# Three score banks and a fourth projection bank, with a new written order, in a cross-attention kernel

## What is computed

```python
q = x @ Wq + bq;  k = ctx @ Wk + bk;  v = ctx @ Wv + bv
scores = einsum('bkgld,bksd->bkgls', q, k) * HD ** -0.5 + mask
attn = softmax(scores, axis=-1)
out = einsum('bkgls,bksd->bkgld', attn, v)      # 8 key heads, 4 query heads each
x = out.reshape(b, l, 1024) @ Wo + bo + x
return (x - mu) * rsqrt(var + 1e-6) * gamma + beta
```

## Time and profile before

| | before |
|---|---|
| median of three executions | 1751.57 us |
| the profiled execution's own time | 1751.32 us |
| its span, first to last instruction | 1749.3 us |
| PE busy | 1602.6 us (92%) |
| DVE, ACT, POOL busy | 83%, 79%, 53% |
| mean granted clock of PE | 0.974 |
| batch 5, from PV 7 of batch 4 to its own PV 7 | 207.67 us |

### The profile page before, as it was taken

One profiled execution on the slowest core, in us unless ns is written; L12 is line 12 of the kernel. 1 busy time (PEld: TensorE's weight loads), 2 busy tenths in 40 slices (PEclk: granted clock), 3 DMA queues, 4 the chain that ended last, 5 costly groups with the idle time before them and its releaser, 6 DMA issues. The chain is left out here.

```text
span 1749.3 us, 38438 instructions
## 1 busy us (share of the span) xinstructions
PE 1602.6 (92%) x14048; PEld 1110.0 (63%) x14048; DVE 1448.7 (83%) x2773; ACT 1385.7 (79%) x3186; POOL 935.7 (53%) x731
## 2 busy tenths in 40 slices
PE   3898879999899989999899998999989999999986
PEld 2665556576566765676576775667666676667654
DVE  4489878789788996889888898789988899788886
ACT  3578868769888787978889789787888878887794
POOL 5426433526754458534675448662585545856382
PEclk8999999999999999999999999999999999999998
DMA  9669987646885578664796567965678646875331
GB/s 178 186 148 227 241 232 199 182 135 168 250 257 144 138 187 286 188 154 122 209 288 185 130 175 192 287 178 127 174 238 252 158 133 170 292 208 150 84 114 67
DMA packets 357292, 325.02 MB, mean 186 GB/s; under 512 B 145776, under 2 KB 248176, under 8 KB 357104
## 3 DMA queue, kind: packets, MB, share of 16 engines
q1 hardware_dynamic: 357104, 322.56, 67.5%
HBM read 244.85 MB, written 83.89 MB: 188 GB/s over the span
## 5 line engine op out<-in xcount | busy, mean ns | idle before, releaser
L1941 PE MATMUL bank<-ring_hi,w_sb 128*128 128x512 f32 x2368 | 785.5, 399 | 32.1 <-issue 19.2
L1725 ACT ACTIVATE probs<-probs,shift 128x512 f32<-128x512 f32 x1024 | 726.9, 713 | 92.1 <-DVE shift L1826 91.0
L1839 DVE STREAM_TRANSPOSE turned_p<-probs 128x2048 f32<-128x2048 f32 x256 | 585.7, 2297 | 154.3 <-PE bank L2021 149.3
L1826 DVE CUSTOM_DVE_ANT_0 probs<-bank,mask_l 128x512 f32<-128x512 f32 x1024 | 643.1, 680 | 56.3 <-PE bank L2001 37.2
L1626 POOL TENSOR_TENSOR w_sb<-w_raw,w_sb 128x512 fp32r<-128x512 f32 x320 | 412.1, 1297 | 413.8 <-ACT w_sb L1682 413.7
L1941 PEld LDWEIGHTS bank<-ring_hi,w_sb 128*128 128x128 f32 x2368 | 444.4, 189 | 149.9 <-issue 42.6
L1941 PE MATMUL bank<-ring_lo,w_sb 128*128 128x512 f32 x1184 | 467.9, 395 | 0.0
L2001 PE MATMUL bank<-k_stack,q_stack 96*128 96x512 f32 x1024 | 358.9, 414 | 12.7 <-DVE shift L1826 10.0
L2021 PE MATMUL bank<-turned_p,v_all 32*32 32x512 f32 x8192 | 307.9, 642 | 65.8 <-DVE turned_p L1839 48.6
L1638 POOL TENSOR_TENSOR ring_lo<-x_t,ring_hi 128x512 fp32r<-128x512 f32 x168 | 214.7, 1291 | 144.9 <-ACT ring_hi L1694 144.4
L2001 PEld LDWEIGHTS bank<-k_stack,q_stack 96*128 96x128 f32 x1024 | 186.1, 189 | 143.3 <-issue 62.9
(11 more groups left out here) (75 smaller groups left out, 933.2 us busy)
## 6 DMA issues: line engine op xcount, KB each, us to landing
w_raw<-w_d SPq DMA_DIRECT2D x144, 256.0 KB, 3.7
q_stack<-q_hi_d SPq DMA_DIRECT2D x128, 256.0 KB, 4.3
w_raw<-in_L_xattn_Wo_dram SPq DMA_DIRECT2D x128, 256.0 KB, 3.0
q_hi_d<-part_hi SPq DMA_DIRECT2D x64, 256.0 KB, 3.9
q_lo_d<-part SPq DMA_DIRECT2D x64, 256.0 KB, 5.0
...
v_all<-v_d SPq DMA_DIRECT2D x256, 64.0 KB, 2.2
...
```

The costliest lines, as they stand in the source:

```text
L1725: nc.scalar.activation(probs[:, st % 2, h, :], probs[:, st % 2, h, :], ACT.Exp, scale=-1.0, bias=shift[:, g % 2, i:i + 1], accum_out=sums[ ...
L1826: nc.vector.tensor_tensor_reduce(out=probs[:, st % 2, h, :], in0=S_ps[h][:, :], in1=mask_l[:, st, :], scale=-1.0, scalar=HIGHEST, op0=ALU. ...
L1839: nc.vector.transpose(turned_p[:, :, :, st, :].rearrange("p j h c -> p h j c"), probs[:, st % 2, :, :].rearrange("p h (j c) -> p h j c", c ...
L1941: mm = nc.tensor.matmul(C[c][:, :], w_sb[:, n_w, (1, 0, 0)[third], d % 4, :], (hi, lo, hi)[third], start=(n == 0), stop=(n == 23))
```

## The change

The PSUM banks are dealt out anew. Scores have three banks (0, 1, 2), used in turn by the running number, and score n waits for the DVE read of score n-3. Bank 3 becomes the projections' own. Projection tiles use bank 3 ("2" in `BANKS`) and, where a window has three or four tiles, bank 4 (and 5) for those in the middle. A window with two tiles has both in bank 3, one behind the other. A PV waits only for the `keep`s of tiles in banks 4 and 5. In the last batch the row products `e` use banks 1, 2, 0 in place of 0, 1, 2, and the last `rbc` uses bank 0 in place of bank 3. `WINDOWS` is unchanged, and each step's work is the same. Nearly every number in `BASE` and `PLACES` differs (about 1,770 lines of the diff), so that all engines have a new order.

```diff
-BASE = {1: 256.32, 2: 463.56, 3: 671.62, 4: 879.00, 5: 1086.39, 6: 1293.78, 7: 1501.17}
+BASE = {1: 252.03, 2: 464.77, 3: 672.77, 4: 880.77, 5: 1088.76, 6: 1296.76, 7: 1504.76}
...
+BANKS = {1: (2,), 2: (2, 2), 3: (2, 0, 2), 4: (2, 0, 1, 2)}
...
+def bank_no(t, what, m, batches):
+    if t < 0:
+        names = WINDOWS["pro"][None if None in WINDOWS["pro"] else -1].split()
+        return (0, 1, 0, 1, 2)[names.index(f"{what}{m}")]
+    names = [xs.split() for xs in WINDOWS[kind_of(t, batches)].values() if f"{what}{m}" in xs.split()][0]
+    return BANKS[len(names)][names.index(f"{what}{m}")]
...
-        S_ps = bank[0:4]
+
+        S_ps = bank[0:3]
+        N_S = 3
         PV_ps = bank[4:8]
-        C = bank[4:6]
+        C = [bank[4], bank[5], bank[3]]
...
-            return bank[m] if what == "e" else C[m % 2]
+            return (bank[1:3] + bank[0:1] + bank[3:])[m] if what == "e" else C[BANK[NB - 1, what, m]]
...
-            return S_ps[3] if (t, g) == (NB - 1, NG - 1) else R_ps
+            return S_ps[0] if (t, g) == (NB - 1, NG - 1) else R_ps
...
-                        if m < 3:
-                            pe.wait_ge(max_done, number(t, NG - 1, 3, m) + 1)
+                        if m < 2:
+                            pe.wait_ge(max_done, number(t, NG - 1, 3, m + 1) + 1)
+                        elif m == 2:
+                            pe.wait_ge(rbc_out, NG * NB)
                         elif m == 3:
-                            pe.wait_ge(rbc_out, NG * NB)
+                            pe.wait_ge(row_kept, len(KEPT))
...
-                    wait(pe, max_done, n - 3)
-                    nc.tensor.matmul(S_ps[h][:, :], q_stack[b][:, h, st * P:(st + 1) * P], k_stack[b][:, :],
+                    wait(pe, max_done, n - N_S + 1)
+                    nc.tensor.matmul(S_ps[n % N_S][:, :], q_stack[b][:, h, st * P:(st + 1) * P], k_stack[b][:, :],
                                      start=True, stop=True).then_inc(score_done, 1)
```

More of the change, by code:

```diff
@@ L160 @@
[L160 to L164 removed]
[8 rows of a table removed]
+            (84.12, 84.64, 85.16, 88.44),
+            (109.65, 110.17, 110.69, 111.9),
+            (134.4, 134.92, 135.44, 136.65),
@@ new lines @@
+        "pv": (79.8, 105.33, 130.08, 156.8, 179.35, 204.83, 229.4, 252.15),
+        "sel": (89.27, 112.7, 137.45, 163.92, 186.72, 214.14, 235.92, 259.52),
+        "rbc": (90.59, 114.01, 138.77, 165.47, 187.8, 216.39, 238.63, 260.83),
+        "rbc_out": (91.31, 114.73, 139.86, 166.4, 188.52, 217.23, 239.8, 261.93),
+        "norm": (102.22, 125.69, 153, 176.24, 200.99, 225.19, 249.04, 272.51),
+        "o_store": (104.54, 127.54, 155.26, 178.98, 202.93, 226.95, 252.36, 275.03),
+        "mask": (32.43, 32.88, 33.33, 33.78),
[8 rows of a table added]
@@ L1018 @@
+        "res o": (3.83, 5.63, 6.08, 6.53),
+        "aggr o": (152.64, 151.59, 152.44, 154.18),
+        "z o": (161.89, 163.05, 172.29, 177.54),
+        "zmul o": (163.17, 169.36, 176.82, 181.72),
+        "zadd o": (165.62, 173.09, 179.27, 191.22),
+        "z_store o": (169.07, 176.54, 182.72, 194.67),
+        "root o": 154.5,
+        "rstd o": 160.99,
+        "res e": (-26.75, -26.3, 59.58, 60.03),
+        "z_store e": (222.94, 231.88, 233.24, 234.6),
     },
@@ L1307, in attention_kernel @@
                     continue
-                c, tile = m % 2, (t, what, m)
+                c, tile = bank_no(t, what, m, NB), (t, what, m)
+                BANK[tile] = c
                 tiles[c] += 1
                 TILE[tile] = tiles[c]
-                if (g, c) not in seen and t >= 0:
+                if (g, c) not in seen and t >= 0 and c < 2:
                     NEW_IN_BANK.add((t, what, m, g))
@@ L1339, in attention_kernel @@
         KEPT = ROWS[:12]
+        for what, m in KEPT:
+            BANK[NB - 1, what, m] = bank_no(NB - 1, what, m, NB)
         assert USES == ROW_BLOCKS and all("e" not in x for x in KEPT)
@@ L1343, in attention_kernel @@
         WINDOW = {new[:3]: new[3] for new in NEW_IN_BANK}
-        FIRST_TILES = [max(n for x, n in TILE.items() if x[0] == -1 and x[2] % 2 == c) for c in range(2)]
+        FIRST_TILES = [max(n for x, n in TILE.items() if x[0] == -1 and BANK[x] == c) for c in range(2)]
         BIASES_AT = [n for n, e in enumerate(STEPS) if e[1] == "w_load"][3] + 1
```

1151 lines of the change are left out of this document (559 added, 592 removed), and 378 rows, old and new, of the table PLACES.

## The result

The changed kernel takes 1766.36 us (median of four executions, 1764.97 to 1768.34). The kernel before takes 1751.26 us (1750.36 to 1754.67) on the same chip. The ratio is 1.0085, with a 95% interval from 1.0067 to 1.0102: slower by 15 us, where 1759 us (7.6 slower) was forecast. The direction and most of the waits in the middle batches were as forecast, and the first two batches were not.

The account below looks back on a forecast made before the run. PE, busy 92% of the span, was taken as the bound, its order being the program's length. Per-batch terms, start and end summed to +6.6 us, rounded up to +7.6, giving 1759 us, range 1751 to 1769.

Parts of the forecast that it names:

- the forecast's own case: Whole program: gains and added waits sum to a slower kernel, 1759 us (1754 to 1764); chance 0.62.
- rival (c): Clock falls once more per batch behind PE's waits, 1.6 us each, so 1769 us; chance 0.17.
- Step "what it removes": Ahead of PVs in batches 1 to 7: the wait for the last tile's `keep` goes, -1.4 us per batch.
- Step 1: Windows of two tiles: the second waits until ACT has read the first from the same bank, +1.0 us per batch.
- Step 2: Turn of batch: with three score banks the seventh score waits for a minimum behind DVE's transposition, +0.5 us per batch.
- Step 3: PV 5, batches 1 to 6: four minima now precede group 5's fourth transposition, +1.1 us each (0 to 2.4).
- Step 4: POOL's order in group 6: wait moves from PV 6 to Q0's tile, as long; 0 us (-0.5 to +1.6).
- Start: Batch 0, PV 5: six matmuls now stand behind the PV where PE waited, -2 us (0 to -4.7).
- End: Last PV: `e2`'s nine matmuls move behind it and PE waits for the transposition, +1.3 us (0 to 2.1).
- Clock: Middle batches: one clock fall per batch behind a long wait, costing 1.6 us, expected again at no difference.
- The rule that was weighed there: PE's clock: cycling through PSUM banks with short idle spells between groups of matmuls makes the clock fall and rise.
- The 1 us by which the sum was rounded up: Whole program: 1 us added to the sum of +6.6, for orders cut to other times, giving +7.6.

Follow-up runs that it names:

- the run with two banks: Changed kernel, but of two tiles in a window the first is summed in bank 4 and only the last in bank 3: 1768.10 us, ratio 1.0097.

## Why the prediction was right and where it was not

- **The number.** 1766.36 us lies within the range as a whole (1751 to 1769), but above the 1754 to 1764 of the forecast's own case, in the part that was there for rival (c), whose 1769 is nearer than the 1759. That the range holds it is luck in part: half of the loss lies where the forecast had a gain.
- **The forecast's own case** came in by its direction and most of its waits. Batch 5 at 209.37 us (about 209), no PV behind a `keep`, PV 5 behind a transposition (1.62; at least 1), Q0 behind POOL (4.07; 3 to 4), a score at the turn (1.17; 0.5 and up to 2). Too high was the wait left at PV 6 (0.37, not 1 to 2), and the idle time ahead of the last PV did not come.
- **Step "what it removes", -1.4 per batch.** Right as a row: the waits are gone. It missed what the new order does with the bank, since it looked for matmuls that cross a PV and found one tile. ACT's `keep` crosses it (it ends 3.2 us behind the start of PV 0 of batch 5), and with the new order on the old banks the program is 111 us longer.
- **Step 1, +1.0 for handovers.** Waits of about this sum came in batch 5 (1.6 us), but only one where it was put: q5's (0.50 for 0.4). o7 was to wait 0.6 and didn't, and q7 and Q0, counted at nothing, waited 0.38 and 0.70. As a price they are wrong as well: taken away, the middle gains nothing, because the bank that replaces them makes PE wait for the PV's copies. The step counted "1.1 of unnamed wait gone" only in POOL's chain; it was probably a second gain from the private bank. It is the 1.1 us of "issue" in the earlier trace rows: kv3's first matmul at 1261.66, 1.15 us behind the start of ACT's four copies of the PV's banks (1260.51), as in the run with two banks. No releaser is named there either.
- **Step 2, +0.5 for three score banks.** The size at the turn was 1.17. That three banks cost so little holds for the new order alone; under the old one they cost 360 us.
- **Step 3, +1.1.** PV 5's lag grows by 1.8 us. The cause given, the four minima ahead of the transposition, is only the wait's last link: with the transposition first, a score waits in its place.
- **Step 4, 0.** PV 6 comes 28.54 us behind PV 5 for 27.62, inside the bounds (-0.5 to +1.6), and the wait did move to Q0's tile. The stretch from PV 6 to PV 7 is 2.1 us shorter, since the lower clock no longer reaches it; the prediction had taken the clock as unchanged. Both together are -1.2 in batch 5. Even so batch 5 loses 1.7 us and not 1.2, since PV 5's lag and the turn of the batch cost more than their terms.
- **Start, -2 forecast for batch 0, +0.6 measured, and +1.2 against +7.0 in batch 1.** This is the failed step. The gain at PV 5 of batch 0 was there and larger (the interval is 5.6 us shorter, for -2 with bounds 0 and -4.7), and where no tile crosses that PV, as in the kernels with the new start on the old banks, it isn't there (the interval is 1.2 us longer). But only that place was looked at, and batch 1 was given the terms of a middle batch. What took the gain back and more is the order elsewhere. The new order of the start has three others, PV 0 of batch 0 (+4.15) and of batch 1 (+4.1) and PV 2 of batch 1 (+7.1), and batches 0 and 1 have tables of their own that the middle batch does not speak for. The kernel with four banks and the new start has all three (3.55, 4.43 and 7.95), so they come with the order and not with the banks. At the first, 1 to 2 us seem to be the loading order. At the third the chain of waits is read from the trace. At the second, moving the transposition did not help. What would mend the last two was not found, so the cause within the order stays open.
- **End, +1.3.** The work moved as said (`e2` behind the PV, nine matmuls from 1733.64 to 1735.91, 2.3 us), and the stretch behind the last PV is 2.55 us longer. But PE then did not wait for the transposition: without the nine matmuls it reaches the PV 1.95 us sooner, and not 0.79. So the end costs 0.6 us. In each of the kernels with the new banks and the new end the PV starts without a wait, as before.
- **Clock.** No further fall in the middle: seven of the eight windows of batch 5 have 1.00, handovers of 0.4 to 0.5 us among them, and the eighth holds the wait of 4.07. The time at the lower level over batches 2 to 7 is 27.2 us in both kernels. This rules out rival (c), a fall more in each batch, for the middle. The rule that was weighed there (the Trainium skill, "TensorE: Matmul & The Clock Gate", section "A second HAM failure mode: psum-queue depth-cycling") does not show in these windows, although the tiles go through bank 3 with short idle spells between. In the start a part of the extra loss is clock: the 13.4 us more at the lower level, nearly all of it in batch 1, cost some 6 us by the prediction's own price (1.6 us for a fall of 3.6), which is an estimate. The fall of 10.2 us shown above begins in a wait of PE.
- **Sizes.** The terms missed by +8.4 us in batches 0 and 1, by +0.8 from there to PV 6 of batch 7 and by -0.7 behind it. The 0.8 would be near 5 but for batch 3, where the kernel before had lost 4 us by itself. The loss does not sit in the first two batches alone, but half of it does. The 1 us by which the sum was rounded up had no row behind it and made the forecast look better by as much.
